# First dense layer of the last row quarter's MLP in two-part fp32r, and its layers and merge placed later

## The chip, the cores and the metric

One core of a Trainium2 chip runs the kernel. The metric is device time in microseconds (us) of one launch. The kernel before takes 591.78 us, the median of three runs (591.65 to 592.2).

## The reference

Two graph layers over a 4096x4096 adjacency matrix `adj` and node features of width 128, each followed by a residual and a layer norm:

```python
def conv(x, a, eps, W, b):                 # twice: (x, W1, b1) and (x2, W2, b2)
    ax = a @ x
    h = ax + (1.0 + eps[0]) * ax
    for i in range(3):
        h = relu(h @ W[i].T + b[i])
    return h
x = layernorm(x + concat(out1, out2) @ Wm.T + bm)
...
A_hat = A + eye; deg = A_hat.sum(1); d = where(deg > 0, rsqrt(deg), 0)
x = layernorm(x + (d[:, None] * A_hat * d[None, :] @ x) @ W.T + b)
```

## The kernel before, in words

**Tiling.** The output rows are four quarters of 1024. For each quarter the kernel walks over 32 tiles of the transposed adjacency matrix (128x1024 fp32, loaded in pairs of 1 MB). Layer 0 (the two convolutions) takes four quarters of 32 tiles, then layer 1 takes the same four again. In both layers fp32 accuracy comes from fp32r products in two parts: ScalarE (ACT) rounds a tile to fp32r (`ahi`, L719), VectorE (DVE) subtracts to get the rest (`alo`, L916), and TensorE (PE) adds hi*hi, lo*hi and hi*lo (L532). A layer-0 tile is 12 matmuls of 512 columns, a layer-1 tile 6. In layer 0 DVE also sums the rows of each tile for the degrees.

**Order.** There is no scheduler: each engine has its own program, written by hand as a loop over tiles, and the engines meet at semaphores. Each engine does its part of tile p and then the extra work that tables of step numbers put at p. Rounded tiles live in a ring of 4 slots, from the fifth tile of layer 1 on of 6, so ACT can be up to six tiles ahead of PE. PE takes the four hi products of a tile first and waits for `alo` only before the last two (`products`, L490 to L534).

**The MLP.** The three dense layers and the merge of a finished quarter are worked on while the next quarter's tiles run. For quarters 0 to 2 (`plan` 0) that is in layer 0; for the last quarter (`plan` 1) it is in the first 32 tiles of layer 1 (`layer1_first`), where PE has only 6 matmuls per tile. ACT evacuates the four banks of the quarter's product into `h` at step 2 (L733). A dense layer is four column chunks m = 0..3, each into its own bank of `pd` (`dense`, L538 to L555). In plan 0 each chunk takes three fp32r matmuls, on the rounded activation `hhi` (ACT, L724 or L745) and its rest (DVE, L938). In plan 1, dense layers 1 and 2 do so too, but dense layer 0 multiplies `h` by `par` in plain fp32. ACT's `relu` (L740) writes `h`, and for plan 1 also `hhi` straight from PSUM (L745). In plan 1 the rest `h_rest` takes the place of `h` in memory. The merge (L562) is 64 small fp32 matmuls, then come DVE's residual `z` (L955), statistics, POOL's power `rstd` (L1241), DVE's `nshift`, `y_scale`, `y_shift`, ACT's `yt` (`last_y`, L782), ACT's `x1hi` (`round_y`, L791) and DVE's `x1lo` (`split_y`, L1070); PE reads these last two from step 32 of layer 1 on.

The tables that set the steps for plan 1 are the second entries of `PE_DENSE` (step 1, 3, 5), `PE_MERGE` (6) and `ACT_RELU` (4, 6, 7), and `DVE_SPLIT_H` (4 and 6, four chunks each). `DVE_RESIDUAL` is merge plus 4, `DVE_AGGREGATE` merge plus 9, `DVE_SHIFT` merge plus 11. DVE's transpose and reduction of the last quarter's row sums (L960, L966) come at step 2, ahead of the split of tile 3.

```python
            def layer1_first():
                for p in range(2 * JB):
                    split_a(p // JB, 1, p % JB)
                    if p < JB:
                        mlp_step(LAST, p, 1)
                        y_step(p, (LAST,))
                        if p in DVE_SPLIT_H:
                            for m in range(M):
                                split_h(LAST, DVE_SPLIT_H[p], m, 1)
```

**Loads.** SyncE's queue loads layer-1 tile pairs into eight buffers in order. The load of pair i waits until DVE has split the pair eight earlier.

Of the kernel before, what the change touches and what calls it, by code (L numbers as in the profile page):

```python
# [31 lines left out]
KB = QW // P  # L32
# [4 lines left out]
CH = QW // CW  # L37
M = 2 * CH
LAYERS = 3
RAW = 4  # L40
RAW2 = 4
SPLIT = 4
SPLIT2 = SPLIT + 2
LN_EPS = 1e-5
LAST = QUARTERS - 1
# [20 lines left out]

PE_DENSE = ({3: 0, 5: 1, 8: 2}, {1: 0, 3: 1, 5: 2})
PE_MERGE = (10, 6)  # L70
DVE_SPLIT_H = {4: 1, 6: 2}
PE_PROJECT = 1
PE_WARM = 8


AHEAD_OF_PE = (SPLIT, SPLIT2)
ACT_EVACUATE = (2, 2)
ACT_RELU = ({k + SPLIT: l for k, l in PE_DENSE[0].items()}, {4: 0, 6: 1, 7: 2})
DVE_RESIDUAL = (PE_MERGE[0] + SPLIT, PE_MERGE[1] + SPLIT)
STATISTICS = (2, 2)  # L80
TB = 32
# [1 line left out]
DVE_AGGREGATE = tuple(k + 1 + KB // s for k, s in zip(DVE_RESIDUAL, STATISTICS))  # L83
DVE_DEGREES = (DVE_RESIDUAL[0] + 1, 13)
DVE_FACTORS = (DVE_AGGREGATE[0] + 2, 16)
ACT_NORM_LAST = 29
DVE_TURN = (5, 2)
DVE_BASE = 10
DVE_BASE_LAST = 20
DVE_SHIFT = tuple(k + 2 for k in DVE_AGGREGATE)  # L90
ACT_NORM = (22, 20)
ACT_COPY_AY = 3
DVE_MAKE_Y = (KB + 4, 2 * KB + 4, 3 * KB + 3, 23)
NORM_BLOCKS = (2, 2)
ACT_ROUND_Y = tuple(k + 1 for k in DVE_MAKE_Y)
DVE_SPLIT_Y = tuple(k + 2 for k in DVE_MAKE_Y)
DVE_SECOND_BASE = DVE_SPLIT_Y[:2] + (JB + 26, 2 * JB + 28)
# [25 lines left out]
def build(nc, a_t, head, early, x12, params, scratch, out):  # L123
    with ExitStack() as ctx:
        def sb(name, shape, dt=F32):
            return ctx.enter_context(nc.sbuf_tensor(name, shape, dt))

        def sem(name):
            return ctx.enter_context(nc.semaphore(name))
# [22 lines left out]
        with ExitStack() as whole:  # L152
            h = whole.enter_context(nc.sbuf_tensor("h", [P, M, CW], F32))
# [9 lines left out]
        par = sb("par", [P, PARAMS])  # L163
# [47 lines left out]
        h_ready = sem("h_ready")  # L211
        hhi_ready = sem("hhi_ready")
        hlo_ready = sem("hlo_ready")
# [55 lines left out]
        def wait(eng, s, value):  # L269

            if not isinstance(value, int) or value > 0:
                eng.wait_ge(s, value)
# [216 lines left out]
        def _(pe):  # L489
# [48 lines left out]
            def dense(q, l, plan):  # L538

                for m in range(M):  # L540

                    if plan == 0:
                        wait(pe, hlo_ready, q * (LAYERS * M) + (M * l + m + 1))
                        passes = ((whi, hhi), (whi, hlo), (wlo, hhi))
                    elif l:
                        wait(pe, hlo_ready, q * (LAYERS * M) + (M * (l - 1) + m + 1))
                        passes = ((whi, hhi), (whi, h_rest), (wlo, hhi))
                    else:
                        wait(pe, h_ready, q * (4 * M) + (M * l + m + 1))
                        passes = ((par, h),)  # L550
                    at = (W1_AT, W2_AT)[m // CH] + l * P
                    for k, (w, a) in enumerate(passes):
                        mm = pe.matmul(pd[:, m, :], w[:, at:at + P], a[:, m, :], start=(k == 0),  # L553
                                       stop=(k == len(passes) - 1))
                    mm.then_inc(dense_done, 1)  # L555

            def merge(q):

                wait(pe, h_ready, q * (4 * M) + 4 * M)
                for k in range(KB):  # L560
                    for b in range(2):
                        mm = pe.matmul(merged[:, k, :], h[:, CH * b + k // 4, (k % 4) * P:(k % 4 + 1) * P],  # L562
                                       par[:, WM_AT + b * P:WM_AT + (b + 1) * P],
                                       start=(k % 4 == 0 and b == 0), stop=(k % 4 == 3 and b == 1),
                                       skip_group_check=True)
                mm.then_inc(merge_done, 1)

            def mlp_step(q, n, plan):
                if n in PE_DENSE[plan]:
                    if n == min(PE_DENSE[plan]):  # L570
                        wait(pe, raw_used, q * PAIRS + PAIRS)
                        wait(pe, z_ready, q)
                    dense(q, PE_DENSE[plan][n], plan)
                if n == PE_MERGE[plan]:
                    merge(q)
# [101 lines left out]
        def _(act):  # L677
# [43 lines left out]
            def round_h(q, l, m):  # L721

                wait(act, h_ready, q * (4 * M) + (M * l + m + 1))
                act.activation(hhi[:, m, :], h[:, m, :], ACT.Copy).then_inc(hhi_ready, 1)  # L724

            def evacuate(q):

                for m in range(M):
                    if m < M - 1:
                        wait(act, ax_done, q * (M - 1) + (m + 1))  # L730
                    else:
                        wait(act, block_used, q * JB + JB)
                    act.activation(h[:, m, :], ps[m][:, :], ACT.Identity,  # L733
                                   scale=gain[:, m // CH:m // CH + 1]).then_inc(h_ready, 1)
# [22 lines left out]
            def mlp_step(q, n, plan):  # L757
                if n == ACT_EVACUATE[plan]:
                    evacuate(q)
                if plan == 0 and n in (ACT_EVACUATE[0] + 1, ACT_EVACUATE[0] + 2):  # L760
                    for m in range(CH):
                        round_h(q, 0, CH * (n - ACT_EVACUATE[0] - 1) + m)
                if n in ACT_RELU[plan]:
                    relu(q, ACT_RELU[plan][n], plan)
                at, size = ACT_NORM[plan], NORM_BLOCKS[plan]
                if plan == 1:
                    if at <= n < at + KB // size:
                        last_y(range(size * (n - at), size * (n - at + 1)))
                elif at <= n < at + KB // size:
                    if isinstance(q, int):  # L770
                        to = lambda k: xn[:, q, k * P:(k + 1) * P]
                    else:
                        to = lambda k: xn[:, bass.ds(q, 1), k * P:(k + 1) * P].rearrange("p o d -> p (o d)")
                    normalise(q + 1, to, xn_ready, range(size * (n - at), size * (n - at + 1)))

            def last_y(blocks):

                if blocks[0] == 0:
                    act.wait_ge(y_scales_ready, 2)
                    act.wait_ge(y_ready, LAST)  # L780
                for k in blocks:
                    i = act.activation(yt[:, k, :], z[:, k, :], ACT.Identity,  # L782
                                       scale=y_scale[:, k:k + 1], bias=y_shift[:, k:k + 1])
                if k == KB - 1:
                    i.then_inc(yt_ready, 1)
# [58 lines left out]
            def layer1_first():  # L844

                for p in range(2 * JB):
# [3 lines left out]
                    if p == ACT_ROUND_Y[LAST]:  # L850
                        round_y(LAST)
                    if ACT_NORM_LAST <= p < ACT_NORM_LAST + KB:
                        normalise(QUARTERS, lambda k: xn[:, LAST, k * P:(k + 1) * P], xn_ready, (p - ACT_NORM_LAST,))
                    quarter_done(0, p - FIRST_ENDS - 1)
# [37 lines left out]
        def _(dve):  # L892
# [40 lines left out]
            def split_h(q, l, m, plan):  # L933

                if plan == 1:
                    wait(dve, h_ready, q * (4 * M) + (M * l + m + 1))
                wait(dve, hhi_ready, q * (LAYERS * M) + (M * (l - plan) + m + 1))
                dve.tensor_tensor((hlo, h_rest)[plan][:, m, :], h[:, m, :], as_f32(hhi[:, m, :]),  # L938
                                  ALU.subtract).then_inc(hlo_ready, 1)

# [77 lines left out]
            def mlp_step(q, n, plan):  # L1018
                if plan == 0:
                    if n in (ACT_EVACUATE[0] + 1, ACT_EVACUATE[0] + 2):  # L1020
                        for m in range(CH):
                            split_h(q, 0, CH * (n - ACT_EVACUATE[0] - 1) + m, 0)
                if plan == 0 and n in ACT_RELU[0] and ACT_RELU[0][n] < LAYERS - 1:
                    for m in range(M):
                        split_h(q, ACT_RELU[0][n] + 1, m, 0)
                if n == DVE_TURN[plan]:
# [50 lines left out]
            def y_step(n, quarters):  # L1077
                for g in quarters:
                    if g < LAST and n == DVE_MAKE_Y[g]:
                        make_y(g)  # L1080
# [66 lines left out]
# [5 lines that stand above are left out]
                        mlp_step(LAST, p, 1)  # L1152
                        y_step(p, (LAST,))
                        if p in DVE_SPLIT_H:
                            for m in range(M):
                                split_h(LAST, DVE_SPLIT_H[p], m, 1)
                    finish_step(0, p - FIRST_ENDS - 1)
                    if p == DVE_SECOND_BASE[2]:
                        second_base(2)
                    if JB <= p and (p - JB + AHEAD2) // KB == 1:  # L1160
                        add_identity(1, p - JB + AHEAD2)
# [145 lines left out]
```

## Time and profile before

| what | value |
|---|---|
| median of three runs | 591.78 us |
| the profiled execution | 591.9 us |
| its span, first to last instruction | 590.1 us |
| PE busy | 582.8 us, 99% |
| DVE busy | 545.2 us, 92% |
| ACT busy | 378.4 us, 64% |
| POOL busy | 28.1 us, 5% |
| TensorE clock granted, mean over the span | 0.997 |

The span leaves out what lies around the first and the last instruction, 1.8 us here. Layer 1 starts on PE at 389.78 us. Times of instructions below are us from the span's start. A matmul's own duration in the trace includes its way through the array: matmuls of 512 columns are 0.39 us long each and start 0.227 us apart when nothing holds them.

### The profile page before, as it was taken

To read this page: it belongs to the slowest core of one execution; us is meant where nothing else is said; L and a number is where in the kernel's file an instruction comes from. 1 tells how busy PE (TensorE), PEld (TensorE's weight loads), DVE (VectorE), ACT (ScalarE), POOL (GpSimd) and SP (SyncE) were. 2 spreads that over 40 slices of the span, in tenths; PEclk is the share of its full clock that TensorE was granted. 3 is DMA by queue.
4 is the path that set the end of the run, shared out by engine and by line. 5 is a ranking of instruction groups with operands and counts; after the bars stand their busy time and mean duration, and the time that the engine had idled before them with its cause. 6 is when DMAs were issued, how large, how long until landed. Compare 5 with 4: busy or idle time off the path is not lost.

```text
span 590.1 us, 7652 instructions
## 1 busy us (share of the span) xinstructions
PE 582.8 (99%) x2676; PEld 485.5 (82%) x2676; DVE 545.2 (92%) x692; ACT 378.4 (64%) x510; POOL 28.1 (5%) x26
## 2 busy tenths in 40 slices
PE   8999999999999999999999999999999999999996
PEld 7788888888888888888888888878888888888885
DVE  6999999998987999898799999997999997989986
ACT  6644537852454773353667336479799799799794
POOL 0000000001100000110000020000200001010011
PEclk9999999999999999999999999999999999999998
DMA  8978565443555454354534365675899998999921
GB/s 329 366 279 288 211 219 209 144 148 143 197 190 193 170 175 148 139 193 178 201 142 148 143 259 187 269 305 203 312 364 396 424 382 337 382 351 353 387 82 72
DMA packets 30731, 141.91 MB, mean 240 GB/s; under 512 B 5488, under 2 KB 6256, under 8 KB 16496
## 3 DMA queue, kind: packets, MB, share of 16 engines
q1 hardware_dynamic: 30128, 139.87, 63.7%
q10 hardware_dynamic: 576, 1.70, 0.7%
q8 instruction: 14, 0.23, 0.2%
q14 instruction: 13, 0.11, 0.0%
HBM read 139.40 MB, written 2.16 MB: 240 GB/s over the span
## 4 chain that ended last, share of the span: by engine, by line
PE 92%; DVE 4%; ACT 1%; DMA 1%; issue 1%; SPq 0%; POOLq 0%; POOL 0%; DVEq 0%
PE ps L532 78%; PE pd L553 6%; PE ps L608 6%; PE pd L562 2%; DVE alo L916 1%; PE pd L594 1%; DMA raw<-early 1%; DVE rowsum L927 1%; DVE rowsum L931 0%; ACT outn L752 0%; DVE x1lo L900 0%; DVE x2s L900 0%; ACT ahi L719 0%; DVE z L1212 0%; ACT ahi_extra L719 0%
## 5 line engine op out<-in xcount | busy, mean ns | idle before, releaser
L719 ACT ACTIVATE ahi<-raw 128x1024 fp32r<-128x1024 f32 x212 | 222.3, 1060 | 159.9 <-PE ps L532 154.0
L916 DVE TENSOR_TENSOR alo<-raw,ahi 128x1024 fp32r<-128x1024 f32 x212 | 256.9, 1220 | 27.0 <-ACT ahi L719 26.0
L532 PE MATMUL ps<-ahi,x2s 128*128 128x512 f32 x512 | 138.3, 389 | 0.0
L532 PE MATMUL ps<-ahi,x1hi 128*128 128x512 f32 x384 | 121.9, 393 | 0.0
L532 PE MATMUL ps<-alo,x1hi 128*128 128x512 f32 x384 | 120.4, 389 | 0.3 <-DVE alo L916 0.3
L532 PE MATMUL ps<-ahi,x1lo 128*128 128x512 f32 x384 | 120.7, 390 | 0.0
L532 PEld LDWEIGHTS ps<-ahi,x2s 128*128 128x128 f32 x512 | 96.1, 188 | 20.0
L532 PEld LDWEIGHTS ps<-alo,x1hi 128*128 128x128 f32 x384 | 72.0, 188 | 15.7 <-DVE alo L916 0.7
L532 PEld LDWEIGHTS ps<-ahi,x1lo 128*128 128x128 f32 x384 | 72.4, 188 | 15.1
L532 PEld LDWEIGHTS ps<-ahi,x1hi 128*128 128x128 f32 x384 | 71.9, 189 | 14.9 <-issue 0.5
L532 PE MATMUL ps<-alo,x2s 128*128 128x512 f32 x256 | 80.3, 389 | 0.0
L927 DVE TENSOR_TENSOR rowsum<-rowsum,raw 128x1024 f32<-128x1024 f32 x60 | 73.1, 1219 | 0.0
L931 DVE TENSOR_TENSOR rowsum<-rowsum,raw 128x1024 f32<-128x1024 f32 x56 | 68.2, 1219 | 0.0
L532 PEld LDWEIGHTS ps<-alo,x2s 128*128 128x128 f32 x256 | 48.0, 188 | 10.0
L916 DVE TENSOR_TENSOR alo_extra<-raw,ahi_extra 128x1024 fp32r<-128x1024 f32 x42 | 50.8, 1221 | 3.9 <-ACT ahi_extra L719 3.6
L719 ACT ACTIVATE ahi_extra<-raw 128x1024 fp32r<-128x1024 f32 x42 | 43.7, 1059 | 2.4 <-PE ps L532 1.8
L740 ACT ACTIVATE h<-pd,par 128x512 f32<-128x512 f32 x48 | 31.8, 695 | 1.0 <-PE pd L553 1.0
L1241 POOL TENSOR_TENSOR rstd<-vareps,halves 128x8 f32<-128x8 f32 (+2 forms) x10 | 20.3, 2026 | 184.0 <-DVE vareps L1121 138.4
L1236 POOL TENSOR_TENSOR degpow<-degc,halves 128x8 f32<-128x8 f32 x4 | 6.6, 1639 | 374.1 <-DVE degpos L981 374.1
L938 DVE TENSOR_TENSOR hlo<-h,hhi 128x512 fp32r<-128x512 f32 x36 | 22.7, 687 | 0.0
L724 ACT ACTIVATE hhi<-h 128x512 fp32r<-128x512 f32 x36 | 22.0, 629 | 0.8
L532 PE MATMUL ps<-ahi_extra,x1hi 128*128 128x512 f32 x64 | 20.0, 389 | 0.0
(102 smaller groups left out, 526.0 us busy)
## 6 DMA issues: line engine op xcount, KB each, us to landing
raw<-a_t SPq DMA_DIRECT2D x108, 1024.0 KB, 4.9
raw<-a_t SPq DMA_DIRECT2D x32, 512.0 KB, 8.6
raw<-early SPq DMA_DIRECT2D x7, 512.0 KB, 7.7
xn<-x SPq DMA_DIRECT2D x3, 1024.0 KB, 8.3
out<-outn ACTq DMA_DIRECT2D x3, 512.0 KB, 6.4
par<-params SPq DMA_DIRECT2D x1, 708.0 KB, 12.9
raw<-head SPq DMA_DIRECT2D x2, 256.0 KB, 3.0
xn<-x SPq DMA_DIRECT2D x1, 512.0 KB, 7.4
```

The lines of the kernel that those rows point to most:

```text
L532: mm = pe.matmul(ps[bank + (CH * (q % 2) if layer else 0)][:, :], block_of(w, n), a[c], start=(n == 0 and k == 0), stop=(n == JB - 1 and k ...
L553: mm = pe.matmul(pd[:, m, :], w[:, at:at + P], a[:, m, :], start=(k == 0), stop=(k == len(passes) - 1))
L562: mm = pe.matmul(merged[:, k, :], h[:, CH * b + k // 4, (k % 4) * P:(k % 4 + 1) * P], par[:, WM_AT + b * P:WM_AT + (b + 1) * P], start=(k ...
L608: mm = pe.matmul(bank, block_of(w, j + t), a[:, at], start=(n == opens and t == 0 and k == 0), stop=(n == closes and t == 1 and k == 2), s ...
L719: act.activation(ring_hi(layer, q, n), raw_tile(layer, n), ACT.Copy).then_inc(hi_ready, 1)
L724: act.activation(hhi[:, m, :], h[:, m, :], ACT.Copy).then_inc(hhi_ready, 1)
L740: act.activation(h[:, m, :], pd[:, m, :], ACT.Relu, bias=par[:, at:at + 1]).then_inc(h_ready, 1)
L916: dve.tensor_tensor(ring_lo(layer, q, n), raw_tile(layer, n), as_f32(ring_hi(layer, q, n)), ALU.subtract).then_inc(lo_ready, 1)
L927: dve.tensor_tensor(rowsum[:, :], rowsum[:, :], tile, ALU.add).then_inc(rowsum_step, 1)
L931: dve.tensor_tensor(to[:, :], rowsum[:, :], tile, ALU.add).then_inc(raw_used, 1)
L938: dve.tensor_tensor((hlo, h_rest)[plan][:, m, :], h[:, m, :], as_f32(hhi[:, m, :]), ALU.subtract).then_inc(hlo_ready, 1)
L1241: pool.tensor_tensor(rstd[:, r], vareps[:, r], halves[:, r], ALU.pow).then_inc(rstd_ready, 1)
```

## The change

Dense layer 0 of the last quarter takes the three fp32r products as the other dense layers do. For that ACT rounds `h` at steps 3 and 4, two chunks each, and DVE splits them at the same steps. PE's dense layers go from steps 1, 3, 5 to 4, 6, 8, the merge from 6 to 10, ACT's relus from 4, 6, 7 to 7, 9, 10. DVE's splits of `h` come two chunks per step. Everything that hangs on the merge goes four steps on, `last_y` from 20 to 24, `round_y` from 24 to 28, `split_y` from 25 to 29. The normalised rows of the last quarter (`ACT_NORM_LAST`) go from 29 to 32.

```diff
-PE_DENSE = ({3: 0, 5: 1, 8: 2}, {1: 0, 3: 1, 5: 2})
-PE_MERGE = (10, 6)
-DVE_SPLIT_H = {4: 1, 6: 2}
+PE_DENSE = ({3: 0, 5: 1, 8: 2}, {4: 0, 6: 1, 8: 2})
+PE_MERGE = (10, 10)
+DVE_SPLIT_H = {3: (0, 0), 4: (0, 2), 5: (1, 0), 6: (1, 2), 8: (2, 0), 9: (2, 2)}
...
-ACT_RELU = ({k + SPLIT: l for k, l in PE_DENSE[0].items()}, {4: 0, 6: 1, 7: 2})
+ACT_RELU = ({k + SPLIT: l for k, l in PE_DENSE[0].items()}, {7: 0, 9: 1, 10: 2})
...
-ACT_NORM_LAST = 29
+ACT_NORM_LAST = 32
...
-ACT_NORM = (22, 20)
+ACT_NORM = (22, 24)
...
-DVE_MAKE_Y = (KB + 4, 2 * KB + 4, 3 * KB + 3, 23)
+DVE_MAKE_Y = (KB + 4, 2 * KB + 4, 3 * KB + 3, 27)
...
-                    elif l:
-                        wait(pe, hlo_ready, q * (LAYERS * M) + (M * (l - 1) + m + 1))
+                    else:
+                        wait(pe, hlo_ready, q * (LAYERS * M) + (M * l + m + 1))
                         passes = ((whi, hhi), (whi, h_rest), (wlo, hhi))
-                    else:
-                        wait(pe, h_ready, q * (4 * M) + (M * l + m + 1))
-                        passes = ((par, h),)
...
-                if plan == 0 and n in (ACT_EVACUATE[0] + 1, ACT_EVACUATE[0] + 2):
+                if n in (ACT_EVACUATE[plan] + 1, ACT_EVACUATE[plan] + 2):
                     for m in range(CH):
-                        round_h(q, 0, CH * (n - ACT_EVACUATE[0] - 1) + m)
+                        round_h(q, 0, CH * (n - ACT_EVACUATE[plan] - 1) + m)
...
-                wait(dve, hhi_ready, q * (LAYERS * M) + (M * (l - plan) + m + 1))
+                wait(dve, hhi_ready, q * (LAYERS * M) + (M * l + m + 1))
...
                         if p in DVE_SPLIT_H:
-                            for m in range(M):
-                                split_h(LAST, DVE_SPLIT_H[p], m, 1)
+                            l, first = DVE_SPLIT_H[p]
+                            for m in range(first, first + CH):
+                                split_h(LAST, l, m, 1)
```

## Rows read from the trace of the kernel before

**Rows 1.** The page, part 1: busy time, share of the span, instructions.

```profile
PE 582.8 (99%) x2676; PEld 485.5 (82%) x2676; DVE 545.2 (92%) x692; ACT 378.4 (64%) x510; POOL 28.1 (5%) x26
```

**Rows 2.** Chain that ended last, in order of time: start us, us, what.

```profile
25.90 1.15 DVE alo L916
...
332.80 59.86 PE ps L532 x264
392.66 3.43 PE pd L553 x8
...
398.82 2.72 PE pd L553 x12
...
411.95 47.64 PE ps L532 x210
...
565.15 6.83 PE ps L608 x30
```

**Rows 3.** Timeline of PE, tile 1 of layer 1: start us, us, instruction, count.

```profile
391.14 0.61 PE L532 MATMUL ps<-ahi,x1hi 128*128 128x512 f32 x2
...
392.04 0.62 PE L532 MATMUL ps<-alo,x1hi 128*128 128x512 f32 x2
```

**Rows 4.** Timeline of DVE, 391 to 399 us.

```profile
391.87 1.23 DVE L960 STREAM_TRANSPOSE outn<-rowsum_all 128x1024 f32<-128x1024 f32 x1
393.14 1.22 DVE L966 TENSOR_REDUCE partial<-outn 128x32 f32<-128x1024 f32 x1
394.27 1.22 DVE L916 TENSOR_TENSOR alo<-raw,ahi 128x1024 fp32r<-128x1024 f32 x1
395.41 1.22 DVE L916 TENSOR_TENSOR alo_extra<-raw,ahi_extra 128x1024 fp32r<-128x1024 f32 x1
396.54 2.54 DVE L938 TENSOR_TENSOR h_rest<-h,hhi 128x512 fp32r<-128x512 f32 x4
```

**Rows 5.** Timeline of PE, a wait on DVE in the first quarter.

```profile
27.09 0.73 PE L532 MATMUL ps<-alo,x1hi 128*128 128x512 f32 x2 [0.31 <-DVE alo L916]
27.66 0.63 PE L532 MATMUL ps<-alo,x2s 128*128 128x512 f32 x2
```

**Rows 6.** Timeline of ACT, 391 to 403 us.

```profile
391.53 1.07 ACT L719 ACTIVATE ahi_extra<-raw 128x1024 fp32r<-128x1024 f32 x1
393.55 0.69 ACT L740 ACTIVATE h<-pd,par 128x512 f32<-128x512 f32 x1 [0.96 <-PE pd L553]
394.14 0.68 ACT L745 ACTIVATE hhi<-pd,par 128x512 fp32r<-128x512 f32 x1
...
401.73 0.76 ACT L745 ACTIVATE hhi<-pd,par 128x512 fp32r<-128x512 f32 x1
```

**Rows 7.** Timeline of DVE, 402 to 440 us.

```profile
402.59 0.69 DVE L938 TENSOR_TENSOR h_rest<-h,hhi 128x512 fp32r<-128x512 f32 x1 [0.36 <-ACT hhi L745]
...
409.03 2.36 DVE L916 TENSOR_TENSOR alo<-raw,ahi 128x1024 fp32r<-128x1024 f32 x2 [2.03 <-ACT ahi L719]
...
437.08 2.35 DVE L916 TENSOR_TENSOR alo<-raw,ahi 128x1024 fp32r<-128x1024 f32 x2
```

**Rows 8.** Timeline of PE: tile 6 after dense layer 2, and tile 26's last two products.

```profile
406.82 0.62 PE L532 MATMUL ps<-ahi,x1hi 128*128 128x512 f32 x2
...
438.57 0.61 PE L532 MATMUL ps<-alo,x1hi 128*128 128x512 f32 x2
```

**Rows 9.** The page, part 6: issues, KB each, median us from issue to landing.

```profile
raw<-a_t SPq DMA_DIRECT2D x108, 1024.0 KB, 4.9
```

**Rows 10.** Busy time by stretch: A:B, us, PE, PEld, DVE, ACT, POOL, PEclk, DMA share, GB/s.

```profile
17.40:27.10 9.70, 9.39 (x43) 7.45 (x41) 9.70 (x10) 5.35 (x6) 0.00 (x0) 1.00 1.00 413
...
585.00:590.00 5.00, 0.11 (x1) 0.00 (x0) 2.04 (x9) 1.47 (x4) 0.69 (x1) 0.67 0.30 107
```

**Rows 11.** Timeline of PE, matmuls near the start of the span.

```profile
5.54 0.63 PE L532 MATMUL ps<-ahi,x1lo 128*128 128x512 f32 x1
5.96 0.63 PE L532 MATMUL ps<-ahi,x1hi 128*128 128x512 f32 x1
```

## The prediction

> **What bounds the kernel.** I read the busy times first: PE is busy for 99% of the span and DVE for 92% [rows 1]. Then the chain of waits in order of time. From 27.1 us to 572 us it consists of PE alone: tiles, dense layers, merges, projections, one behind the other without a gap [rows 2]. So whatever is taken from PE in that stretch is gained, and each wait put into it is lost, one for one, because no later wait is there to swallow it. Third, the timelines of PE, DVE and ACT around 390 to 410 us, side by side, since there the change lies. The reader should look for how long before its use each `alo` is done. In this part of layer 1 that lead hangs on the dense layers: while PE does them it uses no tiles, and DVE and ACT get ahead.
>
> "Tile p" below is the p-th tile of layer 1. Tile 1 starts on PE at 391.14, its last two products, the ones that need `alo`, at 392.04, 0.90 later [rows 3]; six matmuls 0.227 apart make 1.36 a tile.
>
> **Part 1: dense layer 0 in fp32r.** Now it is four fp32 products, eight entries in the chain, 3.43 us; a dense layer of twelve fp32r matmuls takes 2.72 [rows 2]. All of it lies on the path: **-0.71 us**. This is the whole gain that the change can give. One rule of the Trainium skill would make it larger: the page "TensorE: Matmul & The Clock Gate", section "Wait — 56ns, not 53.3ns?", states starts 0.216 us apart for 512 columns at full clock; by that the twelve would take 2.59 and the gain be 0.84. The trace has 2.72 for this form, and that is used.
>
> **Part 2: what the dense layers covered.** Now PE is away for 3.43 us between tiles 1 and 2, for 2.72 between tiles 3 and 4. After the change it runs tiles 0 to 4 without a break, so it comes to tile 3 at 391.14 + 2 x 1.36 = 393.86 and wants its `alo` at 394.77. DVE has nothing to give sooner: its transpose and reduction of the row sums run from 391.87, the split of tile 3 from 394.27 to 395.49 [rows 4], back to back, and nothing of the change lies ahead of them. PE stands from 394.77 to 395.54 (a waiting matmul started 0.04 to 0.05 after the split's end at 27.05, [rows 2, 5]). A restart has a price too: the two matmuls from 27.09 took 0.57 to the next start instead of 0.45 [rows 2, 5], so 0.11 more. First wait: 0.77 + 0.11 = **0.88 us**.
>
> Tile 3 is then done at 396.11, and tile 4's `alo` is wanted at 397.02. On DVE the change puts two splits of `h` between tiles 3 and 4. Such a split holds DVE for 0.60 (four of them in 2.54, the last 0.69 long) [rows 4]. So tile 4's split, now from 395.41, starts at 396.61 and ends at 397.83; PE restarts at 397.88, and with the restart loses 0.87 + 0.11 = **0.98 us**. Tile 4 is done at T = 398.45, where dense layer 0 starts, 1.87 later than without waits. The chunks rounded by ACT don't matter: it has rounded tile 3 when it takes tile 4 at 391.53 and has nothing else to do until 393.55 [rows 6], and with four new roundings of 0.57 to 0.59 each (the pitch of its 512-column instructions, 393.55 to 394.14 [rows 6]) around tile 4 it is done with all at about 394.9. The last two chunk splits are done at 399.05, PE wants the fourth at T + 2.04 = 400.5.
>
> **Part 3: the new place of the split of tile 6.** At step 5 DVE must split chunks 0 and 1 of the first relu before it comes to tile 6. Chunk 0 of dense 0 is out at T + 0.84; ACT does `h`, `hhi`, `h`, `hhi` at 0.57 to 0.59 each, and the second `hhi` ends at about T + 3.3. DVE starts 0.10 after that (401.73 + 0.76 to 402.59) [rows 6, 7], so at T + 3.4, the tile 6 split runs from T + 4.0 to T + 5.25. PE wants it after dense 0 (2.72), tile 5 (1.36) and four products: T + 4.99. Wait 0.31 + 0.11 = **0.42 us**. This one is the least certain: bounds 0 (0.3 us sooner on ACT's side would close it) and 0.75 (0.3 later). I take the middle, which the durations give.
>
> **Part 4: steps 7 to 10.** The same walk gives T + 8.6 for PE at tile 7 with its split done at T + 7.7; for dense layer 2, at T + 11.3, chunk 2's rest at T + 12.3 where PE wants it at 12.7, chunk 3's at 12.9 against 13.3. Tight, but no wait: 0, bounds 0 and 0.3. The merge costs PE the same 3.6 wherever it stands; its `h` is ready 1.4 earlier. ACT has 2.3 us more, DVE 2.4 us more, both hidden if the next part holds.
>
> **Part 5: leads later on.** Before, the lead is smallest at tile 26: split from 437.08 to 438.30, wanted at 438.57, 0.27 [rows 7, 8]. The work that ate it (residual, statistics, `last_y` waiting for `y_shift`, `round_y`) moves four tiles on, so the same place is now tile 30. DVE starts tile 8 at 409.03 after the third relu [rows 7], and 29.27 us later tile 26 is split. After: the third relu ends at T + 15.2, ACT rounds tile 11 in 1.07 [rows 6], DVE starts its split at T + 16.25 = 414.7, with one tile more to do (1.14), so tile 30 is split at 445.1. PE: dense 2 ended at 406.82 before [rows 8], at T + 14.0 = 412.5 after; from there to tile 26's rest 31.75, now one tile more, 33.1, so it wants tile 30's at 445.6. A lead of 0.4 to 0.5: no wait, bounds 0 and 0.6. `x1lo` is done at step 29 of DVE's order, ahead of PE's step 32. The last quarter's `xn` (ACT, steps 32 to 39) is read only at DVE's step 47. POOL's power follows the aggregate by the same distance. On SyncE's queue each load waits for a split eight pairs back, 21.8 us of PE before the use, and takes 4.9 [rows 9]; the splits that release it, and the two transfers of row sums behind them, move by under 1.5 us. All 0.
>
> **Sum.** -0.71 + 0.88 + 0.98 + 0.42 = **+1.57 us**. Against the profiled execution's own 591.9 that is 593.5; the median lies 0.12 below that execution, so the time is 591.78 + 1.57 = **593.35**, 0.27% more. A difference of 0.2%, 1.18 us, is about what measurement of this kernel can tell from none.
>
> **The rivals.**
> *Waits of less than 1.9 us in all* (not slower). The mechanism is that DVE hands over tiles 3, 4 and 6 sooner than I walk it, or the restart price isn't paid. From 1.89 us of waits downward (1.18 + 0.71) the change can't be told from none. Without tile 6's wait and without the two restart prices the sum is -0.71 + 0.77 + 0.87 = +0.93, 592.7; with no wait at all, 591.07, which is still within 0.2%. For it: the third wait hangs on 0.3 us. Against: the first two follow from a queue that was full before. 0.23.
> *The lead runs out at tiles 22 to 31.* DVE and ACT have 2.3 to 2.4 us more to do and the lead there was 0.27. If two more small steps are late by 0.4 each, PE waits for `alo` at tiles 30 and 31, up to 0.6 with restarts, and with the sum above 594.0. For it: the lead there is the smallest that the trace has. Against: the walk gives 0.4 of lead. 0.10.
> *The clock falls.* Granted clock was 1.00 over the wait at 27 us, and 0.67 in the last 5 us, where PE has nothing more to do [rows 10]. At the lower level, 1.2 GHz, matmuls start 0.43 apart (5.54, 5.96) [rows 11] against 0.227. If the waits at tiles 3 and 4 brought that level until dense 0 is done, some 20 matmuls would cost 0.2 each, of which 0.98 hides in the second wait: +3.1, 596.4. The new waits are 0.8 long, much nearer to the one that cost no clock. 0.03. By the Trainium skill, "TensorE: Matmul & The Clock Gate", section "What's actually happening", an idle PE falls back to the lower clock; the trace agrees for the end of the span, not for the short wait.
>
> **How the numbers follow.** The forecast's case (waits of 1.9 to 2.6 us) has 0.62, the rivals 0.23, 0.10, 0.03; 0.02 is left for a gain that I can't price, since PE's own saving ends at 0.71. With some of the forecast's case close to the 0.2% line (a tenth of it may be measured below), slower gets 0.71, same 0.27, faster 0.02. The range reaches down to 592.5 (tile 6 without wait, restarts at nothing, less the runs' scatter) and up to 594.3 (tile 6 at its upper bound with a lost lead).
>
> **What would show it.** The chain should have two new DVE pieces near 395 and 397 us and a short one near 403.5; PE's waits on `alo` L916 in that stretch 1.9 to 2.3 us in all; dense 0 as twelve matmuls in 2.72; the clock at 1.00; no wait between 405 and 570. It would be wrong if PE runs through tiles 3 and 4, or if the waits on `alo` appear at tiles 22 to 31, or on `h_rest` in dense 2.

## The result and the profile after

The changed kernel takes 594.54 us, the median of seven runs (593.88 to 595.26), beside 592.2 us of the kernel before in the same comparison (591.65 to 593.25): ratio 1.0039, 95% interval 1.003 to 1.0048. It is slower by 2.3 us, where 1.57 us was forecast, and the time lies 0.24 us above the stated range.

The page of the changed kernel, its first line, part 1 and the engines' shares in the chain that ended last (part 4), beside [rows 1]:

```profile
span 592.6 us, 7672 instructions
...
PE 583.4 (98%) x2680; PEld 485.3 (82%) x2680; DVE 547.5 (92%) x696; ACT 379.6 (64%) x514; POOL 29.0 (5%) x26
...
PE 67%; DVE 17%; ACT 10%; issue 2%; POOL 1%; DMA 1%; SPq 0%; POOLq 0%; DVEq 0%; ACTq 0%
```

The profiled execution took 594.43 us, of which the span is 592.6. Busy times hardly differ from before; the chain does.

The chain of waits in order of time shows the difference at once. Where it was PE alone from 27 to 572 us [rows 2], it now changes over to ACT and DVE at 387 us and, but for 1.4 us of PE at 398, comes back to PE only at 540 us. Between them stand waits for POOL's power too (`rstd`):

```profile
332.87 54.43 PE ps L532 x240
387.40 1.06 ACT ahi L716
388.47 1.60 ACT h L730 x3
...
395.48 1.29 DVE h_rest L935 x2
396.76 1.15 DVE alo_extra L913
397.96 0.74 PE ps L532 x2
398.69 0.70 PE pd L550 x3
...
404.16 1.90 ACT ahi L716 x2
...
444.24 4.54 DVE alo L913 x4
...
489.87 2.55 POOL rstd L1239
493.05 0.48 ACT outn L749
...
529.48 0.48 ACT outn L749
...
536.10 1.23 DVE alo_extra L913
...
540.46 1.20 PE ps L605 x4
```

So two stretches cost PE time, one at each end of this piece. The first is the forecast one. Timeline of PE in the changed kernel around tiles 3 to 6, to be held against [rows 3]:

```profile
394.38 0.61 PE L532 MATMUL ps<-ahi,x1lo 128*128 128x512 f32 x2
395.62 0.73 PE L532 MATMUL ps<-alo,x1hi 128*128 128x512 f32 x2 [0.62 <-DVE alo L913]
396.18 0.62 PE L532 MATMUL ps<-ahi_extra,x1hi 128*128 128x512 f32 x2
396.65 0.63 PE L532 MATMUL ps<-ahi_extra,x1lo 128*128 128x512 f32 x2
397.96 0.74 PE L532 MATMUL ps<-alo_extra,x1hi 128*128 128x512 f32 x2 [0.68 <-DVE alo_extra L913]
...
401.29 0.61 PE L532 MATMUL ps<-ahi_extra,x1hi 128*128 128x512 f32 x2
...
403.10 0.61 PE L532 MATMUL ps<-ahi,x1lo 128*128 128x512 f32 x2
403.83 0.73 PE L532 MATMUL ps<-alo,x1hi 128*128 128x512 f32 x2
```

And DVE's timeline beside it (compare [rows 4]):

```profile
394.35 1.22 DVE L913 TENSOR_TENSOR alo<-raw,ahi 128x1024 fp32r<-128x1024 f32 x1
395.48 1.29 DVE L935 TENSOR_TENSOR h_rest<-h,hhi 128x512 fp32r<-128x512 f32 x2
396.68 1.22 DVE L913 TENSOR_TENSOR alo_extra<-raw,ahi_extra 128x1024 fp32r<-128x1024 f32 x1
...
402.56 1.22 DVE L913 TENSOR_TENSOR alo<-raw,ahi 128x1024 fp32r<-128x1024 f32 x1
```

Two matmuls take 0.45 from start to start of the next; what is above that before 395.62 is 0.78, before 397.96 0.85, before 403.83 0.28, and after each restart the pair takes 0.11 more. Waits and restarts of 0.89, 0.96 and 0.39, 2.24 in all.

The second stretch was not forecast. Timeline of PE at the end of quarter 2 and the start of the last quarter, tiles 95 and 97 (single matmuls are 0.23 apart):

```profile
536.98 0.39 PE L532 MATMUL ps<-ahi_extra,x1lo 128*128 128x512 f32 x1
537.38 0.50 PE L532 MATMUL ps<-alo_extra,x1hi 128*128 128x512 f32 x1
537.72 0.40 PE L532 MATMUL ps<-ahi_extra,x1hi 128*128 128x512 f32 x1
...
540.00 0.39 PE L605 MATMUL ps<-ahi,x1lo 128*128 128x512 f32 x1
540.46 0.50 PE L605 MATMUL ps<-alo,x1hi 128*128 128x512 f32 x1
540.79 0.39 PE L605 MATMUL ps<-ahi,x1hi 128*128 128x512 f32 x1
```

The waits are short (0.17 and 0.23, each with 0.11 for the restart), so a list of the longest waits doesn't put them forward. A third, in the tail, where matmuls of 256 columns start 0.12 apart, was there before and grew from 0.23 to 0.44.

**How the runs are compared.** The moment at which layer 1 starts on PE moves between executions, whatever the kernel: from 389.1 to 390.6 us in the traces of this study. So I cut each trace at the first matmul of tile 0, of tile 48 (past the stretch that the prediction walked through) and of tile 100 (past the late waits). Each figure is worked out from PE's timeline of the profiled execution.

| kernel | tile 0 to 48 | 48 to 100 | 100 to end | sum |
|---|---|---|---|---|
| before | 79.61 | 74.32 | 46.40 | 200.32 |
| changed | 81.19 | 74.98 | 46.62 | 202.79 |
| fp32 in the new place | 80.46 | 74.89 | 46.58 | 201.93 |
| reduction at step 5 | 79.90 | 74.97 | 46.63 | 201.50 |
| shift later | 81.15 | 75.11 | 46.08 | 202.34 |
| shift later, store aside | 81.17 | 74.32 | 46.07 | 201.56 |
| before, one more DVE op | 79.63 | 75.23 | 46.62 | 201.48 |
| before, two more DVE ops | 79.63 | 76.41 | 46.57 | 202.61 |
| last base at 100 | 81.16 | 74.97 | 47.75 | 203.88 |
| before, late repair | 79.63 | 74.32 | 46.07 | 200.03 |
| early repairs only | 79.24 | 75.05 | 46.63 | 200.92 |
| all waits out | 79.19 | 74.32 | 46.07 | 199.57 |

The changed kernel's 2.47 us are thus 1.58 up to tile 48, as forecast, 0.66 between tiles 48 and 100, and 0.22 in the tail.

The number that explains the rest is the **lead**: from the end of DVE's split of a tile to the start of PE's first product that needs it. At tile 48 it was 5.12 us before and is 4.24 now. Two lines of the changed kernel give it, DVE's split (ends 467.70) and PE's product:

```profile
466.47 1.23 DVE L913 TENSOR_TENSOR alo<-raw,ahi 128x1024 fp32r<-128x1024 f32 x1
```

```profile
471.94 0.61 PE L532 MATMUL ps<-alo,x1hi 128*128 128x512 f32 x2
```

| lead at tile, us | 8 or 11 | 30 | 48 | 68 | 80 | 92 | 94 | 95 | 97 |
|---|---|---|---|---|---|---|---|---|---|
| before | 3.83 | 1.17 | 5.12 | 5.13 | 2.82 | 2.31 | 1.59 | 0.77 | 0.41 |
| changed | 3.64 | 0.27 | 4.24 | 4.24 | 1.93 | 1.41 | 0.69 | 0.05 | 0.05 |
| before, one more DVE op | 3.84 | 1.20 | 5.13 | 3.99 | 1.68 | 1.17 | 0.48 | 0.05 | 0.05 |
| shift later, store aside | 3.65 | 0.27 | 4.25 | 5.14 | 2.52 | 3.40 | 2.36 | 1.54 | 0.60 |
| before, late repair | 3.84 | 1.20 | 5.13 | 5.14 | 2.52 | 3.41 | 2.36 | 1.55 | 0.60 |

(The first column is the first tile behind the third relu, 8 in the kernels with the old places, 11 in the others; 0.05 is a lead that has run out, PE starts as soon as it can. The last three rows are runs that are told below.) The lead of before at tile 95 is 0.77, and the prediction never looked there.

### The profile page after: what moved, and what is told of

The parts are those of the page before. It is cut to its first block, busy times and chain, and to the rows that moved or that the text cites. A ratio compares the mean times of both kernels' runs of the same rounds, so it can differ in the third digit from the quotient of the medians.

```text
span 592.6 us, 7672 instructions
## 1 busy us (share of the span) xinstructions
PE 583.4 (98%) x2680; PEld 485.3 (82%) x2680; DVE 547.5 (92%) x696; ACT 379.6 (64%) x514; POOL 29.0 (5%) x26
## 4 chain that ended last, share of the span: by engine, by line
PE 67%; DVE 17%; ACT 10%; issue 2%; POOL 1%; DMA 1%; SPq 0%; POOLq 0%; DVEq 0%; ACTq 0%
PE ps L532 55%; DVE alo L913 8%; PE ps L605 5%; PE pd L550 4%; DVE alo_extra L913 4%; ACT ahi L716 3%; ACT ahi_extra L716 2%; PE pd L559 2%; ACT outn L749 2%; POOL rstd L1239 1%; ACT h L737 1%; DMA raw<-early 1%; ACT hhi L742 1%; DVE z L1104 1%; ACT outn L806 1%
## 5 line engine op out<-in xcount | busy, mean ns | idle before, releaser
L721 ACT ACTIVATE hhi<-h 128x512 fp32r<-128x512 f32 x40 | 24.4, 630 | 0.8
L532 PE MATMUL ps<-alo_extra,x1hi 128*128 128x512 f32 x64 | 20.3, 393 | 0.7 <-DVE alo_extra L913 0.7
```

The lines of the kernel that those rows point to most:

```text
L532: mm = pe.matmul(ps[bank + (CH * (q % 2) if layer else 0)][:, :], block_of(w, n), a[c], start=(n == 0 and k == 0), stop=(n == JB - 1 and k ...
```

## Experiments

### The old arithmetic in the new place

Theory: the later place of the MLP costs the lead. Rival: the added DVE splits eat it.

```diff
-DVE_SPLIT_H = {3: (0, 0), 4: (0, 2), 5: (1, 0), 6: (1, 2), 8: (2, 0), 9: (2, 2)}
+DVE_SPLIT_H = {5: (1, 0), 6: (1, 2), 8: (2, 0), 9: (2, 2)}
...
+                    elif l:
+                        wait(pe, hlo_ready, q * (LAYERS * M) + (M * (l - 1) + m + 1))
...
+                    else:
+                        wait(pe, h_ready, q * (4 * M) + (M * l + m + 1))
+                        passes = ((par, h),)
```

> The changed kernel with dense layer 0 back in fp32 (no rounding and no split of its input), but all steps where the change put them. Walk: PE still waits about 0.9 us for the split of tile 3, no longer for those of tiles 4 and 6, and dense layer 0 takes 3.43 us again, so PE is +0.9 us against before at tile 48. Theory P (the later place costs the lead: DVE catches up 0.22 us a tile only after the last relu, and has three tiles fewer for it): the lead at tile 48 is as in the changed kernel, 4.2 us, and the late waits at tiles 95 and 97 and in the tail stay, 0.8 us in all; total +1.7 us against before. Theory W (the 2.4 us of added DVE splits eat the lead): the lead at tile 48 is as before, 5.1 us, no late waits; total +0.9 us.

593.76 us beside 592.15, ratio 1.0024 (1.0015 to 1.0033), +1.6 us. Up to tile 48 it is +0.85: tile 3 still waits, tiles 4 and 6 don't, as walked. The lead at tile 48 is 4.35, and the late waits are there, without one added DVE instruction. Waits of this kernel between 530 and 545 us:

```profile
DVE alo_extra L916 <- ACT ahi_extra L719: 0.5, 1, 0.5
PEld ps L608 <- DVE alo L916: 0.5, 1, 0.5
...
PEld ps L532 <- DVE alo_extra L916: 0.3, 1, 0.3
```

So it is the place. The arithmetic fits: after the third relu ACT and DVE start anew, 3.6 to 3.8 us ahead of PE in either schedule. From there DVE needs 1.14 us a tile and PE 1.36. Three tiles fewer until tile 48 are 3 x 0.22 = 0.67 less lead, and the starting lead is 0.19 lower in the changed kernel: 0.86, against 0.88 measured. In this run the starting lead is 3.77, so 0.73, against 0.77 measured. The 2.4 us of added splits lie ahead of the restart, where DVE waits for relus anyway.

### Is a lead ever won back?

In the kernel before, one more instruction on DVE at step 50, whose result nobody reads, and in a second run two of them (`range(2)`).

```diff
+                    if p == 50:
+                        for i in range(1):
+                            dve.tensor_tensor(hhi[:, CH * i:CH * (i + 1), :].rearrange("p m c -> p (m c)"), xn[:, 0, :],
+                                              xn[:, 0, :], ALU.add)
```

> The kernel before with one more 1.14 us DVE instruction at step 50 of layer 1 (its result is used by nobody). Theory L (a lead lost by DVE in the middle of layer 1 is not won back before tiles 95 to 97, where it was 0.8 and 0.4 us): leads from tile 51 on are 1.1 us shorter, PE waits near tiles 95 and 97, +0.9 to +1.2 us against before. Rival R (PE is the bound, DVE has 0.2 us a tile to spare and catches up): 0 us.

> The kernel before with two more 1.14 us DVE instructions at step 50. Theory L: twice the lost lead, and from the point where the smallest later leads are used up each further microsecond of DVE work costs a microsecond: +2.1 to +2.4 us against before (the one-instruction run had +1.2 from tile 0 of layer 1 to the end). Rival (the waits at tiles 95 and 97 are a fixed price for being late at all): again +1.2 us.

One: 593.12 beside 592.15, 1.0015 (1.0006 to 1.0024), 1.16 us from tile 0 to the end, of which 0.91 lie between tiles 48 and 100. Two: 594.65 beside 592.1, 1.004 (1.0027 to 1.0053), 2.29 and 2.09. The first run's waits between 530 and 545 us are again at the split of tiles 95 and 97:

```profile
PEld ps L532 <- DVE alo_extra L916: 0.6, 1, 0.6
DVE alo_extra L916 <- ACT ahi_extra L719: 0.5, 1, 0.5
PEld ps L608 <- DVE alo L916: 0.5, 1, 0.5
```

The lead at tile 95 went from 0.77 to 0.05. By the traces the first instruction cost 1.16 us and the second 1.13. Of the first one's 1.14 us the lead at tile 97 covered 0.36 (0.41 less the 0.05 that remains), and the restart there added 0.11. That makes 0.89, against 0.91 measured between tiles 48 and 100; 0.22 came in the tail. For the second no lead was left, and PE also waited 0.4 us each in front of the projection behind tile 65 and at tile 93. Rival R is out: PE was busy for 99% of the kernel before, and DVE time put in at tile 50 was not won back by tile 97.

The reason isn't that DVE has no time. In the kernel before it stands idle for 6.2 us between its splits of tiles 51 and 95, 5.6 of them waiting for ACT's rounding. But ACT in turn waits for DVE: at tile 67 it stands in front of the normalisation of quarter 0 until `nshift` is there, which DVE makes from POOL's power of what DVE had made before. Where ACT is held by DVE and DVE by ACT, and neither by PE, both stay as late as they were. ACT's timeline of the kernel before and of the changed one:

```profile
490.11 0.88 ACT L752 ACTIVATE outn<-z,nshift,rstd 128x128 f32<-128x128 f32 x2 [0.43 <-DVE nshift L1126]
```

```profile
492.64 0.88 ACT L749 ACTIVATE outn<-z,nshift,rstd 128x128 f32<-128x128 f32 x2 [1.31 <-DVE nshift L1123]
```

The wait is 0.88 longer, the whole of the lost lead.

### Who is late at tiles 92 to 97

In the changed kernel ACT stands 1.41 us in front of its normalisation, then rounds late, and DVE waits for it (timelines of ACT and DVE):

```profile
529.08 0.88 ACT L749 ACTIVATE outn<-z,nshift,rstd 128x128 f32<-128x128 f32 x2 [1.41 <-DVE nshift L1123]
```

```profile
536.10 1.23 DVE L913 TENSOR_TENSOR alo_extra<-raw,ahi_extra 128x1024 fp32r<-128x1024 f32 x1 [0.50 <-ACT ahi_extra L716]
```

Three runs: the changed kernel with the shift and the normalisation a step later; the same with the stores of quarters 0 and 1 moved out of the way; and the changed kernel with DVE's bias addition for the last quarter moved from step 92 to 100.

```diff
-DVE_SHIFT2 = DVE_VARIANCE2 + 2
+DVE_SHIFT2 = DVE_VARIANCE2 + 3
...
-                if n == ACT_NORM2 + KB // 2:
+                if n == ACT_NORM2 + KB // 2 - 1:
```

> The changed kernel with the second norm's shift, and with it ACT's normalisation, one step later (25 to 26 tiles behind), the store in the last of its four steps. Theory A (at tiles 92 to 97 it is ACT that is late: it idles 1.4 us in front of its normalisation until POOL's power and DVE's shift are there, and DVE then waits for ACT's rounding): ACT's idle time goes, the waits of PE at tiles 95 and 97 vanish, -0.6 to -0.85 us against the changed kernel, +1.6 us against before. Theory D (DVE's own work at those tiles, the base of the last quarter and the identities, makes it late): the waits stay, 0 us.

594.37 beside 592.15, 1.0036 (1.0023 to 1.005). Half a miss: the wait at tile 95 went, the gain didn't come. The lead at tile 95 rose from 0.05 to 0.95, but tiles 96 and 97 waited 0.05 and 0.43 with restarts besides, so that tiles 48 to 100 take 75.11. The edit had put the store between the last normalisation and the rounding of tile 96, and ACT stands there:

```profile
535.94 3.90 ACT L716 ACTIVATE ahi<-raw 128x1024 fp32r<-128x1024 f32 x4 [0.47 <-ACT outn L749]
```

The next edit is shown against this run:

```diff
-                if n == ACT_NORM2 + KB // 2 - 1:
+                if n == ACT_NORM2 + KB // 2 - (q == 2):
...
                     quarter_done(before, n)
+                    if q == LAST and n == 2:
+                        store(1)
```

> As the run with the shift a step later, but the store of quarter 1 issued at step 2 of the last quarter and not between ACT's last normalisation and the rounding of tile 96. Theory A (ACT's lateness at tiles 92 to 96 is what PE pays for): the wait at tile 96 goes and the one at 97 nearly, the early waits of 2.2 us stay; 1.6 us over before from tile 0 to the end, 0.4 to 0.5 less than with the store in the way. Theory D: the waits stay because of the four identities and the splits: +2.0 us.

593.19 beside 592.1, 1.0018 (1.0008 to 1.0028), by the traces 1.24 us over before where 1.6 was expected. Tiles 48 to 100 take 74.32, exactly what they took before, although the lead at tile 48 is still 4.25. The early waits are all there. ACT's timeline: its stand in front of the second normalisation is 0.3 shorter than in the changed kernel and comes a tile later, and the rounding of tile 96 starts 1.1 us earlier than with the store in the way, counted from tile 0 (535.57 - 390.35 against 535.94 - 389.58).

```profile
529.63 0.88 ACT L749 ACTIVATE outn<-z,nshift,rstd 128x128 f32<-128x128 f32 x2 [1.12 <-DVE nshift L1125]
...
535.57 1.04 ACT L716 ACTIVATE ahi<-raw 128x1024 fp32r<-128x1024 f32 x1
```

That is one half of it. The other came 30 tiles earlier, at the normalisation of quarter 0, where this kernel's ACT no longer waits for DVE but for PE:

```profile
492.81 1.28 ACT L798 ACTIVATE h<-ps 128x512 f32<-128x512 f32 x2 [0.98 <-PE ps L532]
```

So here DVE's idle time does win the lead back: at tile 68 it is 5.14 in this run, in the late repair of the kernel before and with all repairs, and also in the run before this one, whether it was 4.2 or 5.1 at tile 48. That run lost it again with the store of quarter 0 in ACT's way (4.07 at tile 71, 3.12 at tile 72, as in the changed kernel; here 3.71). No run has the shift later for one of the two quarters alone, so how much of the 0.66 us each half gives back is open.

```diff
-DVE_SECOND_BASE = DVE_SPLIT_Y[:2] + (JB + 26, 2 * JB + 28)
+DVE_SECOND_BASE = DVE_SPLIT_Y[:2] + (JB + 26, 3 * JB + 4)
```

> The changed kernel with DVE's bias addition for the last quarter (1.14 us) at step 100 instead of 92. Theory A (ACT is late there): DVE idles more and PE's waits at tiles 95 and 97 stay, 0 to -0.15 us against the changed kernel. Theory D (DVE's own work is late): the lead at 95 grows by 1.1 us and both waits vanish, -0.6 to -0.8 us.

595.77 beside 592.1, 1.0065 (1.0053 to 1.0077). The waits at tiles 95 and 97 stay (74.97), so DVE's own work there isn't the cause; that part came as theory A said. The size didn't: another 1.1 us appear in the tail, where 0 to 0.15 us less was expected. Waits from 555 to 575 us:

```profile
ACT outn L806 <- DVE nmean L1115: 2.9, 1, 2.9
PEld pd L591 <- ACT h L861: 1.3, 1, 1.3
PE pd L591 <- ACT h L861: 0.8, 1, 0.8
```

DVE's 1.14 us now lie ahead of `nmean`, ACT stands 2.9 us for it (1.7 in the changed kernel) with its copy for the projection behind, and PE waits for that copy. It is the same pattern: ACT, in order, waits for a small DVE result with PE's food queued behind it.

### The first waits

```diff
+DVE_ADD_TURNED = (6, 5)
...
-                if n == DVE_TURN[plan] + 1 - plan:
+                if n == DVE_ADD_TURNED[plan]:
```

> The changed kernel with DVE's reduction of the turned row sums (1.14 us) at step 5 instead of 2, in a stretch where DVE idles about 1 us waiting for the first relu. Theory of the first waits (DVE's full queue ahead of tile 3): the wait for tile 3 vanishes (-0.9 us), that for tile 4 shrinks to 0.6 us and a restart (-0.25 us), that for tile 6 stays; -1.2 us against the changed kernel, so about +1.2 us against before. Rival: DVE gets its lost time back at step 5, tiles 5 and 6 come later by 1.1 us, and little is gained, under 0.4 us.

593.29 beside 592.15, 1.0019 (1.001 to 1.0028). Tile 0 to 48 is 1.29 shorter than in the changed kernel. Tile 3 has a lead of 0.56, and the reduction at its new place, 399.19, ends as the first relu's results arrive. Tile 4 stands 0.47 instead of 0.85, and the tile 6 wait is as it was. PE at tile 4:

```profile
396.98 0.73 PE L533 MATMUL ps<-alo_extra,x1hi 128*128 128x512 f32 x2 [0.31 <-DVE alo_extra L914]
```

The rest, 74.97 and 46.63, is the changed kernel's: the early waits and the late ones have separate causes.

### All together, and each half alone

The version with every repair has the reduction at step 5, the splits of `h` in fours behind tiles 4, 6 and 8, the shift a step later and the store aside:

```diff
-DVE_SPLIT_H = {3: (0, 0), 4: (0, 2), 5: (1, 0), 6: (1, 2), 8: (2, 0), 9: (2, 2)}
+DVE_SPLIT_H = {4: 0, 6: 1, 8: 2}
```

> The changed kernel with all three repairs: the reduction of row sums at step 5, the four-chunk splits behind the splits of tiles 4, 6 and 8, and the shift a step later with the store aside. If both halves of the explanation hold, PE has no wait for tiles 3, 4, 6, 95 to 97, and what is left is the cheaper dense layer: -0.7 us against before, bounds -0.8 and -0.2 (chunk 3 of dense layers 1 and 2 has almost no lead). If it misses a cause: at or above before.

> The kernel before with only the late repair (shift a step later, store of quarter 1 aside). Before it had no PE wait at tiles 95 to 97, so nothing is gained from tile 0 to tile 100: 0 us. In the tail the short wait near 580 us goes as in the repaired runs, -0.3 us. Total -0.3 us against before, so that of the 0.75 us that the version with all repairs gained, 0.4 belong to the changed dense layer. Rival: it gains the whole 0.75 us and the dense layer nothing.

> The changed kernel with the early repairs only (reduction of row sums at step 5, four-chunk splits behind tiles 4, 6, 8). Theory: tile 0 to 48 as in the version with all repairs (79.2 us, 0.4 less than before), but the lead at tile 48 is the changed kernel's 4.2 us, so the waits at tiles 95 and 97 (0.65 us) and the longer tail wait (0.2 us) come back: +0.4 to +0.5 us against before. Rival (the late waits come from the early ones): with no early waits none late, -0.4 us.

All repairs: 591.26 beside 592.1, ratio 0.9983 (0.9975 to 0.9992), faster than both kernels; against the kernel before it gains 0.84 us by the medians and 0.75 by the traces. Tiles 48 to 100 take 74.32 and the tail 46.07. PE's waits that are left between 389 and 470 us, a chunk of dense layer 2 and tile 30:

```profile
PEld pd L551 <- DVE h_rest L938: 0.3, 1, 0.3
PEld ps L533 <- DVE alo L916: 0.2, 1, 0.2
```

Their figures include weight loads. PE's matmuls lose 0.18 at the first (a wait of 0.05, the restart, and 0.01) and 0.09 at the second. These 0.27 are why only 0.42 of the dense layer's 0.71 arrive by tile 48.

The late repair in the kernel before: 592.09 beside 592.4, 0.9992 (0.9983 to 1.0001), not to be told from none by the runs; in the trace 0 up to tile 100, and 0.33 in the tail, as expected. The early repairs alone: 592.53 beside 592.4, 1.0002 (0.9993 to 1.0011), with 79.24, 75.05 and 46.63. By the traces the gain of the first stretch (0.37) is eaten by late waits (0.73) and the tail (0.23), 0.60 over before, though tiles 3, 4 and 6 wait for nothing. The medians differ by 0.13 only, with an interval of -0.4 to 0.65, so here the traces decide. Of the full version's 0.75 the dense layer brought 0.42 and the later shift 0.33, the latter for either kernel. That the sum came near the expected 0.7 is luck: 0.7 was expected of the dense layer alone.

## Why the prediction was right and wrong

The first stretch was right in every term. Dense layer 0 takes 2.76 (398.53 to 401.29, 0.04 of it slow starts behind the wait), for a gain of about 0.7. Forecast waits of 0.88, 0.98 and 0.42 measured 0.89, 0.96 and 0.39, in the forecast places and with the restart price of 0.11; +1.57 forecast by tile 48, +1.58 measured. Part 4 (no wait in steps 7 to 10) held. Part 5's lead at tile 30, 0.4 to 0.5, was 0.27, without a wait. The granted clock stayed at 1.00 in the waits, so the clock rival fell (busy time by stretch of the changed kernel, columns as in [rows 10]):

```profile
389.80:407.00 17.20, 15.78 (x67) 12.06 (x67) 16.15 (x18) 15.36 (x23) 0.00 (x0) 1.00 0.79 304
```

The Trainium skill ("TensorE: Matmul & The Clock Gate", section "What's actually happening") has an idle PE fall back to the lower clock. In waits of 0.8 to 0.9 us the granted clock stayed at 1.00, so these waits don't show it.

The step that failed is the end of Part 5: its "All 0", and with it "no wait between 405 and 570" among the signs. Part 5 followed the lead up to DVE's step 47 and put everything behind it at nothing. It had even worked out that the work behind the third relu moves four tiles on while the relu itself moves three; it checked only that the lead stayed above zero at the nearest narrow place, and not how much of it was gone for the next one. What the runs showed in its place: 0.88 us of lead are lost by tile 48 and, in this kernel, not won back. At tile 97 that is 0.88 less the spare 0.36, plus one restart of 0.11, which makes 0.63; 0.66 were measured between tiles 48 and 100. Another 0.22 came in the tail. 1.58 + 0.66 + 0.22 is the measured 2.47. The lines for it were in the trace of the kernel before: its lead was 0.77 at tile 95 and 0.41 at tile 97. The sentence in the first part that each wait is lost "one for one" held for the waits that were walked through; what it left out is that a change can also make new waits far behind its own place.

The rival that the lead runs out had the mechanism and the wrong place, tiles 22 to 31, and the reason that was given for it, more work on DVE, was wrong too: the old arithmetic in the new place lost the lead as well. The forecast that the change is slower was right, with the range 0.24 us short. Of the signs, two DVE pieces near 395 and 397 us are in the chain, the one near 403.5 isn't. By the terms given for them the chances of slower and same come to 0.69 and 0.29, not 0.71 and 0.27. The chain "PE alone for 545 us" misled: it says what ended last, not how near the second engine is.

Two things stay open. Why the later shift also shortens the tail is only argued: ACT's third wait for the shift, 1.2 us before, is down to 0.3 in the late repair of the kernel before and 0.7 in the first of the runs with the later shift, but that link wasn't tried by itself. And the share of each of the two shifts in the 0.66 us is not separated.

## What to carry to other kernels

Beside the engine that bounds, write down the lead of the engine that feeds it at every narrow place to the end, not only near the change; where the smallest lead is below what the change takes, the rest is paid. Moving a block of work later costs the feeder the tiles of catching up by which its fresh start moves (three here), even with no work added. Idle time of the feeder doesn't mean that it can catch up: ask whom it waits for, and whether that engine waits for the feeder. A result of a few columns that an engine with a fixed order waits for was better asked for a step later here, as long as nothing else (the store) came to stand in its place.

## What was not expected of the hardware

The price of stopping TensorE briefly was the same each time, 0.11 us on the first pair of 512-column matmuls after a wait of 0.05 to 0.85 us, with the granted clock at 1.00. And the start of layer 1 on PE lay between 389.1 and 390.6 us in twelve traces of kernels that are the same up to there, while tiles 48 to 100 of the four kernels without waits there came out at 74.32 us each time: in these traces the scatter arises ahead of layer 1.
